# Eight expert passes instead of nine: the overflow of the busiest expert rides in the last pass

## What is computed

```python
logits = jnp.einsum('bsh,he->bse', x, Wr) + br
probs = jax.nn.softmax(logits, axis=-1)
top_p, top_i = jax.lax.top_k(probs, K)                 # K = 2 of E = 8
cw = jnp.sum(jax.nn.one_hot(top_i, E) * top_p[..., None], axis=-2)
h = jax.nn.relu(jnp.einsum('bsh,ehd->bsed', x, W1) + b1)   # 1024 -> 2048
y = jnp.einsum('bsed,edh->bseh', h, W2) + b2               # 2048 -> 1024
out = jnp.einsum('bseh,bse->bsh', y, cw)
```

## Time and profile before

| | us |
|---|---|
| median of 3 runs (1039.0 to 1039.66) | 1039.09 |
| the profiled execution, its own time | 1042.34 |
| its span, first to last instruction | 1040.6 |
| PE busy | 996.6 (96%) |
| DVE busy | 775.1 (74%) |
| ACT busy | 635.5 (61%) |
| expert passes, from the first unit's matmuls to the end | 589.1 to 1040.6 |

### The profile page before, as it was taken

The page is one execution under the profiler, slowest core; times in us unless marked ns, Lnnn a source line. Parts: engine busy times, 40 slices in busy tenths (PEclk is TensorE's granted clock), DMA queues, the critical chain, the costliest instruction groups (busy, mean ns, idle before and its releaser), DMA issues.

```text
span 1040.6 us, 15023 instructions
## 1 busy us (share of the span) xinstructions
PE 996.6 (96%) x5191; PEld 848.5 (82%) x5227; DVE 775.1 (74%) x1078; ACT 635.5 (61%) x825; POOL 145.0 (14%) x185
## 2 busy tenths in 40 slices
PE   4999999999999999989999899999999999999898
PEld 4898999888889899978788778788787878788675
DVE  7446888867585869767753788888887878788487
ACT  4357777523322133879952667777777787778472
POOL 3003242410001002243320300000000000000013
PEclk9999999999999999989999899999999999999989
DMA  9562342456546763211105499999999999999886
GB/s 313 168 183 83 100 113 70 126 147 173 166 142 182 213 177 117 82 41 42 41 7 201 182 349 381 386 357 371 378 372 374 374 381 359 363 380 385 298 315 232
DMA packets 140508, 237.33 MB, mean 228 GB/s; under 512 B 6908, under 2 KB 48124, under 8 KB 137892
## 3 DMA queue, kind: packets, MB, share of 16 engines
q1 hardware_dynamic: 135780, 225.91, 63.5%
q0 software_dynamic: 1760, 6.37, 1.6%
q10 hardware_dynamic: 2912, 4.34, 1.1%
HBM read 206.56 MB, written 30.03 MB: 227 GB/s over the span
## 4 chain that ended last, share of the span: by engine, by line
PE 78%; DVE 9%; ACT 7%; DMA 3%; issue 2%; SPq 0%; POOL 0%; ACTq 0%; DVEq 0%; POOLq 0%
PE bank L1322 35%; PE bank L971 5%; PE bank L973 5%; PE bank L972 5%; PE bank L985 4%; PE bank L987 4%; PE bank L986 4%; PE bank L1204 2%; DVE wlo L1397 2%; DMA raw<-in_wffn 2%; PE bank L1121 2%; ACT dense L743 2%; PE bank L1048 2%; PE bank L1218 2%; PE bank L1309 1%
## 5 line engine op out<-in xcount | busy, mean ns | idle before, releaser
L1701 DVE TENSOR_TENSOR wlo<-raw,whi 128x2048 fp32r<-128x2048 f32 x72 | 164.6, 2289 | 28.3 <-ACT whi L869 27.9
L869 ACT ACTIVATE a_all<-raw 128x2048 fp32r<-128x2048 f32 x72 | 138.1, 1918 | 52.5 <-DMA raw<-in_wffn 29.0
L869 ACT ACTIVATE whi<-raw 128x2048 fp32r<-128x2048 f32 x72 | 137.9, 1916 | 42.4 <-DMA raw<-in_wffn 23.5
L1397 DVE TENSOR_TENSOR wlo<-raw,whi 128x1024 fp32r<-128x1024 f32 (+1 forms) x72 | 110.4, 1539 | 49.6 <-ACT whi L658 48.4
L658 ACT ACTIVATE whi<-raw 128x1024 fp32r<-128x1024 f32 (+1 forms) x72 | 89.0, 1242 | 90.8 <-PE bank L973 47.7
L1701 DVE TENSOR_TENSOR t_all<-raw,a_all 128x2048 fp32r<-128x2048 f32 x36 | 82.5, 2293 | 40.8 <-ACT a_all L869 40.6
L971 PE MATMUL bank<-a_all,whi 128*128 128x384 f32 x320 | 109.5, 342 | 0.2 <-DVE t_all L1473 0.2
L1322 PE MATMUL bank<-a_all,xg 128*128 128x512 f32 x360 | 106.7, 410 | 1.0 <-DVE t_all L1701 1.0
L973 PE MATMUL bank<-a_all,wlo 128*128 128x384 f32 x320 | 107.2, 335 | 0.0
L972 PE MATMUL bank<-a_all,whi 128*128 128x384 f32 x320 | 107.1, 335 | 0.0
L1322 PE MATMUL bank<-whi,t_all 128*128 128x512 f32 x288 | 100.4, 410 | 0.0
(11 more groups left out here) (276 smaller groups left out, 2041.5 us busy)
## 6 DMA issues: line engine op xcount, KB each, us to landing
raw<-in_wffn SPq DMA_DIRECT2D x144, 512.0 KB
raw<-in_wffn SPq DMA_DIRECT2D x72, 1024.0 KB
raw<-in_wall SPq DMA_DIRECT2D x28, 1024.0 KB
raw<-in_wall SPq DMA_DIRECT2D x32, 512.0 KB
yrows<-zero SPq DMA_DIRECT2D x24, 512.0 KB, 7.0
y_rows<-zero SPq DMA_DIRECT2D x8, 1024.0 KB, 8.7
dense<-yrows SPq DMA_DIRECT2D x8, 512.0 KB, 7.9
y_rows<-dense ACTq DMA_DIRECT2D x16, 256.0 KB, 5.6
```

What stands on the lines that cost most here:

```text
L869: act.activation(hi_ring[u % RAW], raw[:, u % RAW, :], ACT.Copy).then_inc(hi_done, 2)
L1397: dve.tensor_tensor(ring(wlo, k), part(k), ring(whi, k).bitcast(F32), ALU.subtract).then_inc(lo_done, width(k))
L1701: dve.tensor_tensor(lo_ring[u % RAW], raw[:, u % RAW, :], hi_ring[u % RAW].bitcast(F32), ALU.subtract)\
```

## The change

**Eight passes.** The busiest expert is chosen among experts 1 to 7, and it changes places with expert 7: its rows go to the table's last part (`posi` gets an offset, so that it is computed after the choice), its `pick` column to the last place, and an array `order` in memory tells SP which expert's weights belong to a pass. The last pass (`last_expert`) has 192 slots: 128 as before, whose units run as `unit`, and 64 more (`XTRA`).

**The extra 64 slots** hold their token parts side by side, high in columns 0 to 63 and low in 64 to 127 of one 128-column operand. So an `extra_unit` is 8 matmuls of 128 x 512 (4 chunks times w_hi, w_lo). The lower half of the PSUM bank is then the share of the low parts; ACT copies it beside (`eh_copy`, `ey_copy`) and DVE adds the halves (`eh_add`, `ey_add`).

```diff
+            def extra_unit(g, u, b, lhs, final):
+                pe.wait_ge(lo_done, g * F_PIECES + LAYER_PIECES + TURN + 2 * u + 2)
+                w_hi, w_lo = weights(u, RAW - 1)
+                for c in range(4):
+                    for n, w in enumerate((w_hi, w_lo)):
+                        last = pe.matmul(bank[b][:, :].rearrange("p (j n) -> p j n", j=4), lhs[:, c, :], w[:, c, :, :],
+                                         start=False, stop=(final and c == 3 and n == 1))
+                return last
```

**The ring** is 3 places deep in the last pass; the fourth holds the extra slots' tokens and hidden rows (`exT`, `ehid`). A place is free when both shares of its unit have run. `hi_f` now waits for the unit three before:

```diff
-                act.wait_ge(used, g * F_PIECES + LAYER_PIECES + SPLIT + 2 * (u - UP))
-                act.activation(hi_ring[u % RAW], raw[:, u % RAW, :], ACT.Copy).then_inc(hi_done, 2)
+                act.wait_ge(used, g * F_PIECES + LAYER_PIECES + SPLIT + 2 * (u + 1 - depth))
+                act.activation(hi_ring[u % depth], raw[:, u % RAW, :], ACT.Copy).then_inc(hi_done, 2)
```

**PE's order in the last pass.** Units 0 to 2 run for the 128 slots first, then the extra shares of 0 to 2 (ahead of them the transposes of `back`, of the extra tokens and of `back2`). From unit 3 on each unit's two shares stand together:

```diff
+            def last_expert(g):
...
+                bias_row(0, 0, pick2)
+                unit(g, 0, 0, xt[:, 0:4], False, RAW - 1)
+                pe.wait_ge(x_lo, 2 * g + 2)
+                unit(g, 1, 0, xt[:, 4:8], True, RAW - 1)
+                bias_row(1, 512, pick2)
+                unit(g, 2, 1, xt[:, 0:4], False, RAW - 1)
+                pe.wait_ge(ex_lo, 1)
+                pe.wait_ge(back_out, 2)
+                bias_row(6, 0, pick3)
+                extra_unit(g, 0, 6, exT[:, 0:4], False).then_inc(used, 2)
+                extra_unit(g, 1, 6, exT[:, 4:8], True).then_inc(used, 2)
+                bias_row(7, 512, pick3)
+                extra_unit(g, 2, 7, exT[:, 0:4], False).then_inc(used, 2)
+                for b in range(1, 4):
+                    if b >= 2:
+                        bias_row(b % 2, 512 * b, pick2)
+                        unit(g, 2 * b, b % 2, xt[:, 0:4], False, RAW - 1)
+                        pe.wait_ge(eh_added, b - 1)
+                        bias_row(6 + b % 2, 512 * b, pick3)
+                        extra_unit(g, 2 * b, 6 + b % 2, exT[:, 0:4], False).then_inc(used, 2)
+                    if b == 2:
+                        pe.wait_ge(y_copied, 2 * g + 2)
+                    turn_h(g, b - 1)
+                    turn_eh(b - 1)
+                    unit(g, 2 * b + 1, b % 2, xt[:, 4:8], True, RAW - 1)
+                    extra_unit(g, 2 * b + 1, 6 + b % 2, exT[:, 4:8], True).then_inc(used, 2)
```

**Pass 0 is written out** ahead of a loop over passes 1 to 6. On DVE the work on the choice is split:

```diff
+            x_low(0, (0,))
...      14 small operations up to dve.tensor_copy(posi[:, :, :], posf).then_inc(routed, 1)
+            x_low(0, (1,))
+            dve.tensor_tensor(cen, srt, srt[:, :, 0:1].to_broadcast([P, NT, NE]), ALU.subtract).then_inc(cent, 1)
...
+            expert(0, (place_busiest, place_picks, place_rows, place_weights, place_back))
+            with dve.Fori(1, LAST) as g:
+                expert(g)
```

The five `place_` functions (9, 7, 8, 7 and 7 small operations) follow `lo_f(0, 3)` to `lo_f(0, 7)`, one after each. On SP the wait for the scatter and the read of pass 1's tokens move from unit 8 to unit 12 of pass 0, with the read of the 64 extra rows behind it; three registers are loaded ahead of unit 14; and the loop reads `order` twice in each round:

```diff
+            with sp.Fori(1, LAST) as g:
+                expert(g, owner_of(g), lambda: owner_of(g + 1), (g + 1) * C)
```

More of the change, by code:

```diff
@@ L462, in unit, with fetch_rows, expert, owner_of @@
                     sp.dma_start(dst, src[:, :, u % 4, :]).then_inc(raw_in[u % RAW], 32)
-            def expert(g, e, e_next, row):
+            def fetch_rows(g, row):
+                sp.wait_ge(x_turned, 2 * g + 2)
+                sp.dma_start(x_slot, rows[bass.ds(row, SLOTS), :]).then_inc(x_in, 16)
+            def expert(g, e, after, row):
                 for u in range(PRE, UNITS):
                     unit(g, u, e)
-                    if u == UNITS // 2 and row is not None:
-                        sp.wait_ge(x_turned, 2 * g + 2)
-                        sp.wait_ge(scattered, 16 * 2 * NT)
-                        sp.dma_start(x_slot, rows[bass.ds(row, SLOTS), :]).then_inc(x_in, 16)
-                if e_next is not None:
-                    for u in range(PRE):
-                        unit(g + 1, u, e_next)
+                    if u == UNITS // 2:
+                        fetch_rows(g, row)
+                e_next = after()
+                for u in range(PRE):
+                    unit(g + 1, u, e_next)
+            def owner_of(g):
+                return sp.value_load(order[0:1, g:g + 1] if isinstance(g, int) else order[0:1, bass.ds(g, 1)], min_val=0, max_val=NE - 1)
             sp.wait_ge(b_out, 32)
@@ L1326, in combine, with turn_eh @@
+            def turn_eh(b):
+                if b >= 2:
+                    pe.wait_ge(eh_lo, b - 1)
+                pe.wait_ge(eh_added, b + 1)
+                for k in range(4):
+                    last = pe.transpose(bank[2 + b % 2][:, k * XTRA:(k + 1) * XTRA], eh_row[:, b % 2, k * P:(k + 1) * P], ident[0:XTRA, 0:XTRA])
+                last.then_inc(eh_turned, 1)
             def combine(g, i):
+                banks = [bank[(0, 1, 4, 5, 6, 7)[NT * i + t]] for t in range(NT)]
+                pe.wait_ge(ey_added, i + 1)
+                for t in range(NT):
+                    pe.matmul(banks[t][:, :], backT2[:, t, :], ey_row[:, i * 512:(i + 1) * 512], start=True, stop=False)
@@ L1368, in expert @@
                             combine(g, 0)
-                if final:
-                    combine(g, 1)
+                combine(g, 1)
             pe.wait_ge(b_in, 16)
-            with pe.Fori(0, NE) as g:
-                expert(g, False)
+            expert(0)
+            with pe.Fori(1, LAST) as g:
+                expert(g)
             pe.wait_ge(busy_ready, 4)
@@ L1377, in _ @@
             with pe.If(more > 0):
-                with pe.Fori(NE, NE + MORE) as g:
-                    expert(g, False)
-            expert(more * MORE + NE, True)
+                with pe.Fori(LAST, LAST + MORE) as g:
+                    expert(g)
+            last_expert(more * MORE + LAST)
         @block.vector
@@ L1832, in _ @@
-            link(dve.tensor_tensor(val[:, 0, :], val[:, 0, :], val[:, 1, :], ALU.add))
-            for t in range(NT):
-                last = dve.tensor_scalar(back[:, t, :], slot1[:, :], val[:, 0, t:t + 1], w8[:, 0, t:t + 1], ALU.is_equal, ALU.mult)
-            last.then_inc(g_ready, 1)
-            with dve.Fori(0, NE) as g:
-                expert(g, False)
+            link(dve.tensor_scalar(small[:, 152:153], small[:, 62:63], float(C), float(-LAST * C), ALU.mult, ALU.add))
+            link(dve.scalar_tensor_tensor(out=moved, in0=eid[:, :], scalar=float(LAST), in1=owner, op0=ALU.is_equal, op1=ALU.subtract))
@@ new lines, in place_back @@
+            def place_back():
+                for t in range(NT):
+                    last = dve.tensor_scalar(back[:, t, :], slot1[:, :], val[:, 0, t:t + 1], w8[:, 0, t:t + 1], ALU.is_equal, ALU.mult)
+                last.then_inc(g_ready, 1)
+                link(dve.tensor_scalar(val[:, 1, :], val[:, 0, :], float(-SLOTS), None, ALU.add))
+                for t in range(NT):
+                    last = dve.tensor_scalar(back2[:, t, :], slot1[:, 0:XTRA], val[:, 1, t:t + 1], w8[:, 0, t:t + 1], ALU.is_equal, ALU.mult)
+                last.then_inc(g_ready, 1)
```

355 lines of the change are left out of this document (242 added, 113 removed).

## The result

On one chip the kernel after took 1045.22 us (median of 8 runs, 1041.65 to 1049.33) and the kernel before 1039.32 (8 runs): ratio 1.0052, 95% interval 1.0028 to 1.0076. The forecast was 1025.9, range 1021 to 1032. The profiled execution of after has a span of 1046.2 us, 18.8 over the 1027.4 of the prediction's sum.

| step | predicted | profile after | more |
|---|---|---|---|
| first matmul of pass 0 | 589.1 | 590.2 | 1.1 |
| to the `turn_x` of pass 0 | 41.9 | 43.9 | 2.0 |
| six passes, `turn_x` to `turn_x` | 288.0 | 293.6 | 5.6 |
| last `turn_x` to the start of the last pass, P | 9.0 | 13.1 | 4.1 |
| P to the end | 99.4 | 105.4 | 6.0 |

The account below looks back on a forecast made before the run. PE's own work, 48.0 us a pass, was taken as the bound. Last-pass start 927.5 + pass 0's 0.5 + last pass 99.4 = 1027.4 against 1040.6, -13.2; from 1039.1 that gives 1025.9 us, range 1021 to 1032.

Parts of the forecast that it names:

- A pass taken away is worth 48.0 us: Passes run on PE's own work, 48.0 us each, so removing one of nine saves 48.0 us.
- Loop, passes 1 to 6: "Cost 0": In the looped passes SP's two register loads per pass were to cost nothing, leaving PE's chain unbroken.
- Slack 1.1 in each turn: In the weight ring a place turns round in 10.9 us, for four units of 3.0, leaving 1.1 us spare.
- The start of the last pass: Most of the old 8.3 us loss there was to be hidden; jumps counted were ACT's 7.2, SP's 5.31, DVE's 0.5.
- (a): Last pass, after the first three units: PE waits 0.9 us for ACT's late return from its jump and the following copies.
- (b): Last pass, ahead of turn_eh(0): PE waits 2.3 us for DVE's eh_add(0).
- (d): Last pass, unit 8: turn_eh(3) comes after one share only, so PE waits 1.5 us for eh_add(3).
- (c): Last pass, blocks 1 and 2: eh_add ends at 30.4 against 31.0 and 40.8 against 41.4, so no wait.
- (e): Last pass, combine(0): both inputs ready, ey_add(0) ending near 71 and PE arriving at 77, so no wait.
- The clock: Rival: PE's clock falls in the last pass, giving 1029, with two falls 1032; 20 in 100 together with a longer start.
- The scatter: Pass 0: POOL's scatter starts 9 us later but is done 10 us before SP asks for it; no cost.
- The slower one: Rival: SP's register loads come into the path of the looped passes' weight ring, 1040 to 1044 us; 4 in 100.

Follow-up runs that it names:

- k1: After with the choice of the busiest made earlier, the last pass reordered, PE's pass 0 in its loop to a register bound, no PE block: 1024.08 us, ratio 0.9847.
- j1: After, with PE alone running pass 0 in its loop again and without PE's conditional block: 1034.97 us, ratio 0.9946.
- e1: After, with PE's conditional block of further rounds left out: 1038.96 us, ratio 0.9990.
- j2: Before, with one more pass written into PE's conditional block alone, never entered: 1045.03 us, ratio 1.0039.
- the three kernels of 2519: PE programs counted at 2519 instructions: before (1039 to 1041 us), before with a later scatter (1046.54), before with a dead pass on DVE alone (1039.78).
- e2: After, with the scatter's row numbers made early, ahead of lo_f(0, 1), without exchanging the two experts' rows: 1041.22 us, ratio 1.0010.
- e4: After, with DVE's five place_ pieces of pass 0 behind units 0, 2, 5, 8 and 11 instead of 0 to 4: 1045.09 us, ratio 1.0043.
- f1: After, with SP's register loads taken out of the loop, so that pass g takes expert g's weights: 1045.47 us, ratio 1.0050.
- g1: After, with one more wait on PE ahead of pass 1 so that the ring of loads stands full: 1055.41 us, ratio 1.0150.
- i1: After, without the conditional blocks of all five engines and the register loads that decide on them: 1039.00 us, ratio 0.9987.
- e3: After, with the last pass's first extra copy and addition one unit earlier and turn_eh(3) behind unit 8's extra share: 1037.66 us, ratio 0.9971.

## Why the prediction was wrong

- *"A pass taken away is worth 48.0 us"* held: k1 has one pass less, its steps are 48.0, and it is 1.5% faster.
- *Loop, passes 1 to 6: "Cost 0".* This step failed, by 5.6 us (4 to 5 by the pairs j1 against e1, and j2 against before). I looked for a cost in what SP does in the loop, and it was in none of the changed instructions: with PE's longer program the loads are slower everywhere in the kernel. The ring that kept up with 48.0 us a pass takes 48.2 to 49 with packets 1 to 2% longer, and so becomes the bound. The step that hid this is "DMA, ACT and DVE only have to keep up" with its "Slack 1.1 in each turn": the slack was worked out from the length of one transfer, but the queue of the loads holds its engines for 99.0% of the loop in the kernel before already. That PE's program does it is shown in both directions (j1, j2); how is not. Between 2519 and 2558 in the table the effect is there or not, and nothing in the runs tells a threshold of length from a placement in memory that the length shifts.
- *The start of the last pass.* The prediction took ACT's, SP's and DVE's jumps from rows and left out PE's, 0.35 us before. It became 6.47, and the loss 4.1 us. e1 shows it. What the Trainium skill says ("Runtime: NRT & Kernel Launch", Instruction fetch mechanics), that a taken branch to a target outside the pages held waits for a fetch, was weighed for ACT's jump, and that one did become short, so that wait (a) vanished. By that rule each jump over such a block is short or long as its target happens to fall, PE's too. The traces agree in that PE's takes 0.35 us in the three kernels of 2519 and 6.2 to 6.5 in the longer ones that have it; where a page ends no run shows. It should have been a term for all engines.
- *(b) 2.3 and (d) 1.5 us.* Right in place, releaser and size (2.24 and 1.71). (c) and (e), no wait, were right.
- *The clock.* One fall or two, or a longer start, was a rival at 20 in 100. There were three in the last pass, behind pauses of 3.8, 2.24 and 1.71 us; the work behind them lost 1.8 (2.3 + 6.6 us for the opening and 24 matmuls, 1.6 + 5.5 in k1), 1.8 and 1.6 us, 5.2 together. The rest of P to the end, under 2 us, is PE's work taken too small (`combine(0)` 5.54 for 5.1). The prediction's sum priced a pause at its own length, and its rival asked only of (a) and (b) whether the clock falls; the clock added 1.6 to 1.8 us to each. But a pause doesn't always bring a fall: the same pause ahead of `turn_eh(3)`, 1.69 to 1.72 us, was followed by a fall in five kernels (after, e1, e2, e4, f1) and by none in three (g1, i1, j1), and PE's pause of 3.46 us ahead of j2's last pass by none either. PE's windows behind it in i1 and j2:

```profile
987.60:990.60 3.00, 2.99 (x15) 1.00 0.98 365
```

```profile
982.60:985.60 3.00, 3.00 (x15) 1.00 0.82 170
```

  So the length of a pause alone doesn't tell, and what else decides is open.
- *The scatter.* The prediction gave its later start no term, and pass 0 took 2.0 us more than the 41.9 of the sum (within the "+3" of its bounds, but not for the reasons given there). I asked whether the rows would be there when SP wants them, and they were. What the scatter collides with was the error: the two loads in the chain of pass 0 took 9.9 and 10.2 us instead of 6.5, and the pause that this made brought a fall of the clock with it. e2 shows both.
- *The rivals.* The slower one, at 4 in 100, named the right place, the ring in the loop, and with 1040 to 1044 us nearly the right time, but the wrong agent and too much slack. f1 refutes the agent.

What stays open is how PE's program acts on the loads, where the limit lies, and whether as much dead code on another engine would do the same.

## What to carry to other kernels

Count a written-out pass as a cost even where it runs no extra work: here it made the loads slower, and a jump of 0.35 us into one of 6.5. Where a ring of loads just keeps up with PE, lengthen the program without running anything more and time that; it takes one run and tells whether a small slack will hold. A pause of PE of some 2 us can cost nearly as much again in the clock (here 1.6 to 1.8 us where the clock fell, nothing where it didn't), so reorder until only waits like e3's 0.72 us are left, and look for a moved transfer's price in the transfers that it now meets.

## What was not expected of the hardware

- Dead code on PE alone slows other engines' loads: 0.119 us instead of 0.104 for a packet of 2 KB between 150 and 250 us, 0.091 instead of 0.090 in the looped passes, +0.4% in time. One pass of dead code on DVE, a sixth as long, does not (0.101 and 0.090 us).
- A pause of PE of 1.71 us was followed by a fall to 1.2 GHz that cost 1.6 us more, in some kernels and not in others; one of 3.46 us in j2 by none; one of 0.72 us in e3_last_order cost 0.2.
- The ring's lead changes slowly: g1 took two passes to lose it. The step behind a disturbance says little about the loop's own pace.
